# Eight of 64 basis chunks move from the build of the adjacency matrices to the end of the first layer

## What is computed

```python
def _L0_gnn_ref(h, img_feats, batch_ids, src, dst, ...):
    logits = (jnp.tanh(node_proj[:, None, :] + img_proj_n) @ Wa)[..., 0] + ba[0]
    att = jax.nn.softmax(logits, axis=1)
    h1 = h @ Wn + bn
    neigh = jax.ops.segment_sum(h1[src], dst, num_segments=N)
    msg = neigh + img @ Wim + bim
    return jax.nn.relu(jnp.concatenate([msg, h1], axis=1) @ Wap + bap)

def rgcn_gate_layer(x, row, col, edge_type, basis, att, gate_w, root, bias):
    w = jnp.einsum('rb,bio->rio', att, basis)
    ...
    return agg + x @ root + bias

x = _layernorm(x + _L0_gnn_ref(...), axis=-1)
x = _layernorm(x + _L1_gnn_ref(...), axis=-1)   # two rgcn_gate_layers, basis1 and basis2
x = _layernorm(x + _L2_gnn_ref(...), axis=-1)   # five gin layers
x = _layernorm(x + _L3_gnn_ref(...), axis=-1)
```

## Time and profile before

| | us |
|---|---|
| median of three runs (1823.96 to 1830.86) | 1828.7 |
| profiled execution | 1824.01 |
| its span, first to last instruction | 1822.2 |
| PE busy | 1759.3 (97%) |
| DVE busy | 859.9 (47%) |
| ACT busy | 580.5 (32%) |
| DMA, 157.27 MB, mean | 86 GB/s |

### The profile page before, as it was taken

One profiled execution on the slowest core, in us unless ns is written; L12 is line 12 of the kernel. 1 busy time (PEld: TensorE's weight loads), 2 busy tenths in 40 slices (PEclk: granted clock), 3 DMA queues, 4 the chain that ended last, 5 costly groups with the idle time before them and its releaser, 6 DMA issues.

```text
span 1822.2 us, 22269 instructions
## 1 busy us (share of the span) xinstructions
PE 1759.3 (97%) x7346; PEld 850.8 (47%) x7346; DVE 859.9 (47%) x1877; ACT 580.5 (32%) x1185; POOL 11.0 (1%) x37
## 2 busy tenths in 40 slices
PE   5989888999999999999999999999999999999998
PEld 3555555533334444444444444444544444444444
DVE  7888886479883221112122225334252433594123
ACT  2555544466774211222110001232323323232000
POOL 1000000000000000000000000000000000000000
PEclk9999999999999999999999999999999999999999
DMA  7999989810302401000011115300000010021111
GB/s 181 267 263 274 256 236 241 310 35 13 132 24 74 164 0 47 0 1 24 0 40 42 35 35 227 159 1 29 1 1 29 1 41 0 1 82 58 35 47 47
DMA packets 46692, 157.27 MB, mean 86 GB/s; under 512 B 8726, under 2 KB 10670, under 8 KB 38006
## 3 DMA queue, kind: packets, MB, share of 16 engines
q1 hardware_dynamic: 44704, 146.43, 26.5%
q10 hardware_dynamic: 1878, 9.44, 1.4%
HBM read 120.19 MB, written 35.65 MB: 86 GB/s over the span
## 4 chain that ended last, share of the span: by engine, by line
PE 83%; DMA 7%; DVE 6%; issue 2%; DVEq 1%; ACT 1%; POOL 0%; POOLq 0%
PE psum L1541 31%; PE psum L1527 31%; PE psum L1782 7%; DMA hs<-in_L_gnn_basis 4%; PE psum L1455 2%; PE psum L1422 2%; PE psum L1732 2%; DMA adj<-in_L_gnn_basis 2%; PE psum L1629 2%; PE psum L1616 1%; PE psum L1454 1%; PE psum L1493 1%; PE psum L1708 1%; DVE hs L710 1%; DMA wb<-in_L_gnn_Wf 1%
## 5 line engine op out<-in xcount | busy, mean ns | idle before, releaser
L1541 PE MATMUL psum<-hs,adj 128*128 128x512 f16 x2880 | 636.2, 379 | 0.0
L1527 PE MATMUL psum<-wb,xt 128*128 128x512 f32 x1056 | 458.1, 593 | 0.8 <-DVE hs L1011 0.8
L1541 PEld LDWEIGHTS psum<-hs,adj 128*128 128x128 f16 x2880 | 281.2, 98 | 330.7 <-issue 11.0
L1527 PEld LDWEIGHTS psum<-wb,xt 128*128 128x128 f32 x1056 | 198.6, 190 | 245.9 <-issue 244.2
L1292 ACT ACTIVATE ua<-ua 128x512 f32<-128x512 f32 x60 | 37.7, 629 | 314.9 <-DVE ua L1088 181.1
L1084 DVE SCALAR_TENSOR_TENSOR vt<-psum,scl,xt 128x512 f32<-128x512 f32 x60 | 44.8, 746 | 192.7 <-PE psum L1541 192.7
L1019 DVE TENSOR_TENSOR vt<-psum,adj 128x512 f32<-128x512 f32 x24 | 16.6, 692 | 249.3 <-PE psum L1527 249.3
L1527 PE MATMUL psum<-adj,xt 128*128 128x512 f32 x288 | 130.1, 594 | 0.0
L1782 PE MATMUL psum<-hs,adj 128*128 128x512 f32 (+1 forms) x312 | 123.8, 559 | 0.0
L1455 PE MATMUL psum<-hs 128*128 128x192 f32 x404 | 99.7, 329 | 0.0
L1280 ACT ACTIVATE lnst<-lnst,bcol 128x1 f32<-128x1 f32 x24 | 7.1, 295 | 280.1 <-DVE lnst L988 270.5
(11 more groups left out here) (253 smaller groups left out, 1715.7 us busy)
## 6 DMA issues: line engine op xcount, KB each, us to landing
hs<-in_L_gnn_basis SPq DMA_DIRECT2D x38, 960.0 KB, 11.4
adj<-in_L_gnn_basis SPq DMA_DIRECT2D x26, 960.0 KB, 12.9
aw_scratch<-xt ACTq DMA_DIRECT2D x12, 768.0 KB, 10.0
adj<-aw_scratch SPq DMA_DIRECT2D x1, 9216.0 KB, 36.5
x_scratch<-adj SPq DMA_DIRECT2D x24, 256.0 KB, 2.4
hs<-x_scratch SPq DMA_DIRECT2D x24, 256.0 KB, 2.6
ts_scratch<-adj SPq DMA_DIRECT2D x2, 2304.0 KB, 17.8
as_scratch<-adj SPq DMA_DIRECT2D x1, 4608.0 KB, 16.7
```

Source lines behind the costliest of these rows:

```text
L1527: x = pe.matmul(psum[:, bank, :], xt[:, i, k, :], w[:, k, :], start=first and k == 0, stop=last and k == 3)
L1541: x = pe.matmul(psum[:, i % 2 + (4 * half if own else 0), :], adj[:, m, j, P * i:P * i + P], hs[:, t, half, j, :], start=n == 1 or (own an ...
```

## The change

The build takes the first 56 chunks (`IN_BUILD`), spread over the first 95 windows; two buffers are left from chunk 44 on and not from 52. The last eight chunks, four pairs, all of the second sub-layer, are done in rounds 8 to 11 of the first layer. Their two buffers (`late_basis`) lie where `second` and `halves_at[0]` were, and the copy (`late_mixed`) lies in the quarter of `halves_at[1]`, where the thrown-away squares now go too; so ACT's squares also wait for the last dots. ACT issues the loads of a pair from its own queue: the first ones behind the squares, the others when PE has used the buffers (`late_copy`, before the copy of tile 0, 3, 6 in its loop). PE does a pair behind the attention's product of the round (`late_pair`). SP stores a pair in four pieces at four places among its loads and stores of x. The start of the second layer waits for the last copy (`late_read`), and the reload of `adj_flat[2]` for the last stores (`late_out`).

```diff
--- before.py
+++ after.py
@@ -127,7 +127,9 @@
         def first_of(n, g):
 
             return halves_at[n % 2][0][:, g, :] if n % 2 == 0 or g < 3 else halves_at[1][1][:, 0, :]
-        squares_in = adj_flat[2][:, 0:2 * D].bitcast(BF16).rearrange("p (c n) -> p c n", c=2)
+        squares_in = adj_flat[2][:, 16 * D:18 * D].bitcast(BF16).rearrange("p (c n) -> p c n", c=2)
+        late_basis = [part(adj_flat[2], 8192 * k, [4 * D]) for k in range(2)]
+        late_mixed = part(adj_flat[2], 16384, [D])
         squares4 = img.bitcast(BF16).rearrange("p (c n) -> p c n", c=4)
         wim = part(adj_flat[2], 18432, [8, D])
         wb_top = part(adj_flat[2], 18432 + 4096, [4, D])
@@ -181,7 +183,9 @@
         basis = [flat[:, 0:4 * D * 2].bitcast(F32), lay(4 * D, F32)]
         for m in (1, 2):
             basis.append(adj[:, m, NT - 3:NT, :].rearrange("p j n -> p (j n)")[:, 0:4 * D * 2].bitcast(F32))
-        FAR_CHUNKS = 52
+        LATE = 8
+        IN_BUILD = 64 - LATE
+        FAR_CHUNKS = 44
 
         def basis_of(n):
 
@@ -193,7 +197,7 @@
 
         def follower(n):
 
-            return min([m for m in range(n + 1, 64) if basis_of(m) == basis_of(n)], default=None)
+            return min([m for m in range(n + 1, IN_BUILD) if basis_of(m) == basis_of(n)], default=None)
         aw_stage = xt[:, :, :, :].rearrange("p a b d -> p (a b d)")[:, 0:2 * NT * P].rearrange("p (k j d) -> p k j d", k=2, j=NT)
         span = lay(2 * 2 * NW, F32, "p (f h w) -> p f h w", f=2, h=2)
         spant = lay(2 * NW, F32, "p (h w) -> p h w", h=2)
@@ -281,6 +285,8 @@
         basis_in = [sem(f"basis_in{k}") for k in range(4)]
         comb_out = [sem(f"comb_out{k}") for k in range(4)]
         act_done = sem("act_done")
+        late_in = [sem(f"late_in{k}") for k in range(2)]
+        late_ps, late_read, late_out = sem("late_ps"), sem("late_read"), sem("late_out")
         attw_ready, att_all, picked = sem("attw_ready"), sem("att_all_ps"), sem("pick_ready")
         bb_in = [sem(f"bb_in{k}") for k in range(2)]
         fin = sem("fin")
@@ -315,8 +321,8 @@
                 here += [("turn", s, q - 1)]
             if u == NW - 1:
                 here += [("turn", BLOCKS - 1, n) for n in range(6)]
-            if u % 3 != 2:
-                n = 2 * (u // 3) + u % 3
+            if u < NW - 1 and (u + 1) * IN_BUILD // (NW - 1) > u * IN_BUILD // (NW - 1):
+                n = u * IN_BUILD // (NW - 1)
                 here.append(("basis", n // (CH // 2), n % (CH // 2)))
             for what in here:
                 by_window[u].append((len(side),) + what)
@@ -399,7 +405,7 @@
                 a, b = X_GROUPS[g]
                 sp.dma_start(x_first[:, a:b, :], ins["x"][P * a:P * b, :].rearrange("(k p) d -> p k d", p=P)).then_inc(x_in[g], 16)
 
-            for n in range(CH):
+            for n in range(IN_BUILD):
                 l, c = n // (CH // 2), n % (CH // 2)
                 lot = lot_of[("basis", l, c)]
                 if n == FIRST_SMALL:
@@ -410,7 +416,7 @@
                 if follower(n):
                     sp.wait_ge(side_ps, lot + 1)
                     load_chunk(follower(n))
-                    if follower(n) == CH - 1:
+                    if follower(n) == IN_BUILD - 1:
                         x_load(2)
                 if c % 2 == 0:
                     continue
@@ -431,7 +437,7 @@
             sp.wait_ge(typed_summed, BLOCKS)
             sp.dma_start(wf, ins["L0_gnn_Wf"].rearrange("(k p) n -> p k n", p=P)).then_inc(weights["wf"], 16)
             for k in range(4):
-                sp.wait_ge(comb_out[k], 64 * 9)
+                sp.wait_ge(comb_out[k], 64 * (1 + IN_BUILD // 8))
             sp.dma_start(img[0:RG, :], ins["L0_gnn_img_feats"][0]).then_inc(weights["img"], 16)
             sp.dma_start(wi, ins["L0_gnn_Wi"].rearrange("(k p) n -> p k n", p=P)).then_inc(weights["wi"], 16)
             sp.dma_start(wb[:, 1, :, :], ins["L0_gnn_Wn"].rearrange("(k p) n -> p k n", p=P)).then_inc(weights["wn"], 16)
@@ -494,16 +500,28 @@
             sp.wait_ge(u_ps, tick(0, NT - 1))
             relation(0, 0)
             sp.dma_start(as_dram, adj_flat[0]).then_inc(weights["as_out"], 16)
-            for i in range(2, 10):
+            def late_stores(p):
+
+                sp.wait_ge(late_read, p + 1)
+                for q in range(4):
+                    sp.dma_start(combs[1][q, (CH - LATE) % (CH // 2) // 2 + p, :, :], late_mixed[32 * q:32 * q + 16, :]).then_inc(late_out, 16)
+
+            for i in range(2, 9):
                 first_load(i)
+            sp.wait_ge(halves_used, LOTS)
+            first_load(9)
             first_store(0)
             first_store(1)
             first_load(10)
+            late_stores(0)
             for i in range(2, 5):
                 first_store(i)
             first_load(11)
-            for i in range(5, 9):
+            late_stores(1)
+            first_store(5)
+            for i in range(6, 9):
                 first_store(i)
+            late_stores(2)
             sp.wait_ge(acc_ps, tick(0, NT - 1))
             sp.wait_ge(weights["as_out"], 16)
             roots(0)
@@ -512,6 +530,8 @@
             sp.dma_start(gate_rows, ins["L1_gnn_gate_w2"].rearrange("r d o -> o r d").broadcast_to([P, 2, D])).then_inc(gate_rows_in, 16)
             for i in range(9, NT):
                 first_store(i)
+            late_stores(LATE // 2 - 1)
+            sp.wait_ge(late_out, 64 * (LATE // 2))
 
             for k in range(2):
                 sp.wait_ge(y_out[k], 16 * 6)
@@ -1243,6 +1263,7 @@
                     softmax_exp(1)
             softmax_exp(2)
             act.wait_ge(halves_ready, LOTS)
+            act.wait_ge(halves_used, LOTS)
             act.wait_ge(weights["l1a"], 32)
             for t in range(2):
                 for c in (0, 2):
@@ -1253,6 +1274,25 @@
                 a, b = STD_GROUPS[k]
                 act.wait_ge(var_ready, b)
                 act.activation(first_st[:, 2, a:b], moments[:, a:b, 1], ACT.Sqrt, bias=bcol[:, 5:6]).then_inc(std_ready, 1)
+
+            act.wait_ge(sq_ready, n_sq[0])
+
+            def late_loads(p):
+
+                for k in range(2):
+                    c = (CH - LATE) % (CH // 2) // 2 + p + 16 * k
+                    act.dma_start(late_basis[k][0:120, :], bases[1][:, c * (4 * D):(c + 1) * (4 * D)]).then_inc(late_in[k], 16)
+
+            late_loads(0)
+
+            def late_copy(p):
+
+                act.wait_ge(late_ps, 2 * p + 2)
+                if p < LATE // 2 - 1:
+                    late_loads(p + 1)
+                if p:
+                    act.wait_ge(late_out, 64 * p)
+                act.activation(late_mixed, psum[:, 2 + p % 2, :], ACT.Copy).then_inc(late_read, 1)
 
             for i in range(NT + 1):
                 if i < NT:
@@ -1266,6 +1306,8 @@
                                    bias=first_st[:, 4, i:i + 1], scale=first_st[:, 3, i:i + 1]).then_inc(y_ready, 1)
                 if i:
                     j = i - 1
+                    if j % 3 == 0:
+                        late_copy(j // 3)
                     act.wait_ge(t_ps, tick(0, j))
                     act.wait_ge(y_ready, tick(0, j))
                     act.activation(xt[:, j, :, :].rearrange("p k n -> p (k n)"), psum[:, 6 + j % 2, :], ACT.Copy).then_inc(t_cp, 1)
@@ -1571,6 +1613,8 @@
 
                     pe.wait_ge(acc_read, tick(r - 1, NT - 1))
                     pe.wait_ge(o_read, tick(r - 1, NT - 1))
+                if (r, i) == (1, 0):
+                    pe.wait_ge(late_read, LATE // 2)
                 if r in (1, 2):
                     if i >= 2:
                         pe.wait_ge(u_lo, tick(r, i - 2))
@@ -1683,6 +1727,16 @@
                     dots()
             softmax_back(0)
 
+            def late_pair(p):
+
+                if p >= 2:
+                    pe.wait_ge(late_read, p - 1)
+                for h in range(2):
+                    pe.wait_ge(late_in[h], 16 * (p + 1))
+                    for v in range(4):
+                        x = pe.matmul(psum[32 * v:32 * v + 32, 2 + p % 2, :], attw[0:120, 1, 1 - h:33 - h], late_basis[h][0:120, D * v:D * v + D], start=h == 0, stop=h == 1, skip_group_check=True)
+                    x.then_inc(late_ps, 1)
+
             def turned_back(j):
 
                 pe.wait_ge(y_ready, tick(0, j))
@@ -1709,6 +1763,8 @@
                 if i == 7:
                     softmax_turn(2)
                 dots()
+                if i >= 8:
+                    late_pair(i - 8)
                 for j in BACK_LAST.get(i, ()):
                     turned_back(j)
             turned_back(NT - 2)
```

## The result

| | us |
|---|---|
| before, median of 4 runs beside it (1823.96 to 1830.86) | 1828.01 |
| after, median of 4 runs (1837.35 to 1840.96) | 1839.03 |
| ratio, with its 95% interval | 1.0057 (1.0041 to 1.0073) |
| profiled execution after, its span | 1840.96, 1839.1 |

The change costs 11 us by the medians; the forecast was 14.5 and the direction slower. The two profiled executions are 16.9 us apart (spans 1822.2 and 1839.1): the one of before took 1824.01 us, about as short as the shortest of its four runs, the one of after was the longest of its four. Which part of the kernel makes that difference is one of the questions of the experiments.

What follows compares the result with a forecast made beforehand. Build bound by DVE's pace, end of the first layer by PE; -7 + 11.1 + 1.5 + 6.4 + 2.5 = +14.5 us, so 1843 us against the median of 1828.7; range 1830 to 1853.

Steps and rivals of the forecast that it cites:

- What bounds the build: Build of the first layer: it runs at DVE's pace, with the loads just below becoming the bound.
- Rival (b): Build: paced by its loads after all, so 36 us go there and the kernel takes 1814 us; chance 0.06.
- The gain of 7 us: Build: eight chunks leaving it save 7 us of waits, at least 4 and at most 12.
- 10 x 0.98: Build: DVE's waits for PE that stay, 0.98 us in each of ten windows with a fourth tile.
- I take 5.4: Build: 5.4 us taken as gain out of 7.7 us of DVE waits over the floor.
- The first late pair, 11.1 us: Tile 8's round: second chunk there at 571.0, 1.3 us of it for other traffic; cost 11.1 us, 2.1 being lots.
- the 8 to 10 that I gave as the sign of being right: First late pair: one PE wait of 8 to 10 us, named for the load, would show the forecast right.
- Rival (a): Late loads: they come at full rate, two 1 MB loads in 6.8 us; kernel 1834 us; chance 0.20.
- The clock, 1.5 us (0 to 2): Behind the first pair's hole: PE's granted clock 0.62 for 4 us, costing 1.5 us of full-rate work.
- The other three pairs, 6.4 us of lots: Later rounds: each pair adds 2 x 1.06 = 2.1 us to a PE round without a gap, 6.4 us.
- Waits of the later pairs, 2.5 us: Later pairs: PE waits for loads 0.5 us at pairs 1 and 2, 1.5 before pair 3; 0 to 12.
- Rival (c): Later rounds: loads land late, PE waits 3 to 4 us in each of three; kernel 1852 us; chance 0.14.

Runs made afterwards that it cites:

- the first trace: The study's own profiled execution, no edit: of the kernel before 1824.01 us; where the late part is discussed, of the changed kernel 1840.96 us.
- the second trace of the changed kernel: The changed kernel run again without an edit: 1838.9 us, ratio 1.0060; profiled execution 1838.5 us.
- the shorter build: The changed kernel without its late loads, lots and copies, so the last eight chunks are never done: 1820.6 us, ratio 0.9955.
- third and fourth trace: The kernel before, unchanged, profiled two more times to see a longer execution: 1829.8 and 1831.9 us.

## Why the prediction was right, and where it wasn't

**What bounds the build: right.** The kernel with half the loading settles that the loads don't pace it but only disturb it. That DVE's own pace is the bound is read from its timeline; no run changed DVE's work. Rival (b), a build paced by loads, would have given 30 us and more there.

**The gain of 7 us: right in size (7.6), by luck.** I took it from the first trace, with 8.1 us of waits, and 5.4 + 1.6 us of them as gain. Against that very trace the gain is only 2.4 us up to the mark (3.4 in the second trace of the changed kernel), and the last lot of the build comes 2.0 and 3.5 us earlier, not some 7. The waits for chunks did go, all of them, and the end gained 1.7 us (4.13 to 2.39). The failing step is the floor of "10 x 0.98" and with it "I take 5.4". With no chunk late, DVE's waits for PE don't fall to 9.8 us: they are 12.9 in ten places in the shorter build and 13.4 in the changed kernel. Only 4.1 to 4.6 us of the 17.5 could go, and not 7.7. They are also not all in windows with a fourth tile, since there are ten of those and 14 waits. Besides, the idle time for "issue" at one line of DVE rose by 5.2 us. It is 4.1 to 5.1 us in the four traces of before and 8.4 to 9.8 in every trace in which PE has no wait for chunks, half loads among them. I read this as a pause that stays hidden as long as chunks are late; no run shows it. The size came out right because a second error made up for the first: the first trace's waits are not those of a median run. In the third and fourth trace they are 12.6 and 15.5 us, and the mark comes 5.8 and 7.9 us later. The prediction did set the sum beside the profiled execution and the median, but it moved the whole 4.7 us over as if they lay outside the change. By the table they lie in the build, in the term that the change removes. A median that is well above the profiled run should have been read as a range for that term.

**The first late pair, 11.1 us: measured 10.6, by two errors that cancel.** The loads were expected 7.1 and 11.6 us after the issue, plus 1.3 us for the traffic of x, and came at 7.2 and 11.7. The 1.3 us weren't paid by the loads; the small transfers paid. A store of x issued at 559.60 landed after 8.0 us:

```profile
x_scratch<-adj SPq DMA_DIRECT2D x1, 256.0 KB, 8.0
```

In their place 0.9 us were lost because the second lot ran at the lower clock. So PE's two waits make 7.4 us, under the 8 to 10 that I gave as the sign of being right. Issued 13 us earlier against the mark, the loads cost no wait at all. Rival (a), loads at the rate of other 1 MB loads, is out. Its 6.8 us for two such loads is the median of the two landings, so the second came later than that; they moved at 392 GB/s:

```profile
688.00:690.00 2.00, 2.00 (x11) 0.89 (x10) 0.00 (x0) 0.00 (x0) 0.00 (x0) 1.00 1.02 392
```

The Trainium skill's page "DMA: Bandwidth & Descriptors" (Anatomy of one DMA) gives by its fit, which is for DMAs issued by GpSimd, an estimated 6.5 us for the two loads; these two, issued by ACT, took 11.7.

**The clock, 1.5 us (0 to 2): too small in the first trace.** It was 0.50, the lower of TensorE's two levels, over most of the hole and for the work behind. Slowed were the second lot (1.93 for 1.06 us), the transposes (1.97 for 1.09) and part of the aggregation (6.65 for 5.34 in the first trace, 5.43 for 5.34 in the second): 3.1 and 1.8 us. The 0.9 us of the lot are already in the 10.6. The aggregation starts 11.2 us late in the first trace (570.97 against 562.18 - 2.4), and its own part is 1.3: hole and clock together are 12.5, where I had 11.1 + 1.5 = 12.6. In the second trace they are 11.0. The total of the first trace is that near only because the unpaid 1.3 us of traffic stood against the clock. What the Trainium skill's page "TensorE: Matmul & The Clock Gate" (Part 1) says of an idle array, that it goes to 1.2 GHz and comes back after work, the trace shows here too, with 0.50 from 560 us on and 1.00 from 574.

**The other three pairs, 6.4 us of lots: too large by 0.8.** A pair is 1.86 us, since its lots overlap: 3 x 1.86 = 5.6. The term that was off is "2 x 1.06".

**Waits of the later pairs, 2.5 us: too large, and half wrong in kind.** In the first trace one of the rounds, from 585.26 to 599.46, takes 14.20 us and not 12.98; the others have nothing beyond lots and clock. Of these 1.2 us a load made 0.24; 0.55 were a late tile of ACT:

```profile
598.96 0.66 PE L1746 MATMUL psum<-ident,adj 128*128 128x128 f32 x4 [0.55 <-ACT adj L1305]
```

I had priced the traffic on the loads alone, and it is the stores of x beside them that suffer. The kernel with early loads against the one without loads puts this at 2.8 us. Rival (c), late loads in every round, didn't happen.

**The sum.** The late part was put at 21.5 and is 12.5 + 5.6 + 1.2 = 19.3 in the first trace, 17.9 in the second. With the gain of 7.6 that gives 10 to 12 us, and the medians say 11.0; the forecast of +14.5 was above it by the gain (0.6), the lots (0.8) and the later waits (1.3), against the second trace also by the first pair (1.6). The range of 1830 to 1853 holds the measured 1839.0. (In the chances, "within" is 0.20 for (a) and 0.06 for a tenth of the forecast, 0.26 and not 0.24.)

**What stays open.** Why DVE's idle time for "issue" at one line nearly doubles once no chunk is late: it is in all six traces without such waits, but nothing here takes it apart. What makes the stretch behind the build differ, from 240.4 to 244.0 us in the twelve traces. And which of the late part's two sides, PE's lots or the crowded DMA engines, a better place would avoid; no place for the lots outside the stage that PE bounds was tried.

## What to carry to other kernels

Work taken out of a stage that another engine paces gives back only the waits that it caused (here 7.6 us, most of them by its loads), and costs its own length where it lands if that stage is bound by its engine (here 6.5 us for eight lots on PE). A load must be issued its own landing time ahead of the first wait for it; here two issues that came 13 us earlier in ScalarE's program were worth 9.4 us. And when runs of a kernel scatter by far more than those of its variants, the profiled run is one sample of the very wait that is being priced: look where the scatter is before the sum is made.

## What the runs showed of the hardware that I had not expected

- Loads of 120 rows of 8 KB moved at 209 to 225 GB/s with the DMA engines busy at a share of 0.93 to 1.00, on ACT's queue as on SP's (217); two 1 MB loads of another shape moved at 392.
- Beside them a 256 KB store took 9.7 us to land by the median, and 2.1 us without them, though it is issued on another queue.
- The same hole of some 10 us cost 3.1 us of clock in one execution and 1.8 in the next.
- 33 runs of the kernel before cover 16 us (1821.3 to 1837.0), and ten others 12 us; 12 runs with half the loading cover 3.7 us, and 12 with eight chunks fewer 5.5 us.
